# Softmax maxima written to DRAM element by element, and the order of the other tiles moved, in a fused feed-forward/attention kernel

## What is computed (reference, cut)

```
x = x + 0.5 * ffn(layernorm(x))        # 8 experts, top 2, and a shared expert
x = x + attn(layernorm(x))             # 16 heads of 64, see below
x = x + 0.5 * ffn(layernorm(x))
# attn: h = layernorm(x) * ln_scale + ln_bias
#   c_q = h @ w_down_q.T ; c_kv = h @ w_down_kv.T          (128 wide)
#   q, k, v = heads of c_q @ w_up_q.T, c_kv @ w_up_k.T, c_kv @ w_up_v.T ; rotary embedding on q, k
#   out = softmax(q k / 8) v, heads joined, @ w_out.T, + residual
```

## Time and profile before

| | |
|---|---|
| runs (3), device time | 4095.92 us median, 4093.1 to 4099.3 |
| profiled execution, device time | 4098.04 us |
| its span, first to last instruction | 4096.1 us |
| mean granted TensorE clock | 0.988 of full speed |
| busy share of the span | PE 95%, DVE 70%, ACT 62%, POOL 72% |
| DMA | 300.36 MB, 192772 packets |

### The profile page before, as it was taken

How to read it: one execution, slowest core, us unless ns; L and a number is a source line. 1 busy time by engine, 2 the same in 40 slices (tenths; PEclk the granted TensorE clock), 3 DMA queues, 4 the chain that set the end, 5 groups by cost and what they waited for, 6 DMA issues and landing times. The chain is left out here.

```text
span 4096.1 us, 65749 instructions
## 1 busy us (share of the span) xinstructions
PE 3897.4 (95%) x24908; PEld 2207.7 (54%) x24908; DVE 2849.5 (70%) x3796; ACT 2536.2 (62%) x3191; POOL 2932.8 (72%) x1632
## 2 busy tenths in 40 slices
PE   7999979999999999999999999999999999989999
PEld 6888834444444444444444444444444444478888
DVE  5656567777777776777778777767776777565563
ACT  4455446766766676667666766766676666645544
POOL 3444448878877897888788878878887888634443
PEclk9999989999999999999999999999999999999999
DMA  3233221111211221121122212211211121142331
GB/s 123 99 124 109 81 93 53 60 55 59 83 53 53 71 66 53 61 81 53 53 66 76 63 53 66 68 50 60 86 55 53 58 79 62 33 145 76 125 114 63
DMA packets 192772, 300.36 MB, mean 73 GB/s; under 512 B 50328, under 2 KB 100937, under 8 KB 191817
## 3 DMA queue, kind: packets, MB, share of 16 engines
q1 hardware_dynamic: 192456, 296.17, 22.3%
HBM read 201.20 MB, written 26.73 MB: 56 GB/s over the span
## 5 line engine op out<-in xcount | busy, mean ns | idle before, releaser
L1088 DVE TENSOR_REDUCE atNM<-atPS 128x2 f32<-128x1024 f32 x1024 | 1225.7, 1219 | 452.8 <-PE atPS L899 450.1
L1029 ACT ACTIVATE atPT<-atPS 128x1024 f32<-128x1024 f32 x1024 | 1014.0, 1024 | 773.1 <-PE atPS L920 766.7
L1187 POOL TENSOR_TENSOR atACC<-atACC,atPT 128x1024 f32<-128x1024 f32 x510 | 1238.7, 2429 | 89.3 <-ACT atPT L1029 39.1
L931 PE MATMUL atPO<-atPT,atV 128*64 128x512 f32 x4096 | 1014.2, 602 | 0.0
L1187 POOL TENSOR_TENSOR atACC<-atPT 128x1024 f32<-128x1024 f32 x255 | 606.6, 2379 | 262.8 <-PE atOT L953 181.7
L1020 ACT ACTIVATE atPS<-atSH 128x1024 f32<-128x1024 f32 x683 | 687.4, 1023 | 50.8 <-DVE atNM L1088 34.0
L920 PE MATMUL atPS<-atQH,atKL 64*128 64x512 f32 x2048 | 459.9, 445 | 66.3 <-DVE atPS L1094 51.7
L931 PEld LDWEIGHTS atPO<-atPT,atV 128*64 128x64 f32 x4096 | 259.0, 136 | 456.5 <-issue 433.1
L899 PE MATMUL atPS<-atKH,atQH 64*128 64x512 f32 x2048 | 444.0, 431 | 10.0 <-ACT atQH L1009 7.9
L1094 DVE COPY atPS<-atSH 128x1024 f32<-128x1024 f32 x341 | 418.7, 1228 | 37.9 <-DMA atSH<-atMD 11.4
L920 PE MATMUL atPS<-atQH,atKH 64*128 64x512 f32 x2048 | 406.6, 393 | 0.0
(11 more groups left out here) (278 smaller groups left out, 6461.5 us busy)
## 6 DMA issues: line engine op xcount, KB each, us to landing
atSH<-atMD SPq DMA_DIRECT2D x128, 512.0 KB, 4.3
atVT<-atR SPq DMA_DIRECT2D x508, 128.0 KB, 2.1
f1GB<-f1GD SPq DMA_DIRECT2D x128, 256.0 KB, 6.7
f2GB<-f2GD SPq DMA_DIRECT2D x128, 256.0 KB, 6.8
atRSUM<-atRD SPq DMA_DIRECT2D x126, 256.0 KB, 4.0
X<-x SPq DMA_DIRECT2D x4, 1024.0 KB, 6.0
XS<-x SPq DMA_DIRECT2D x16, 256.0 KB, 3.6
x<-X SPq DMA_DIRECT2D x16, 256.0 KB, 2.3
```

What stands on the lines that cost most here:

```text
L931: ins = pe.eng.matmul(PO[HI[h], :], V[n % 2][:, j, HI[h]], PT[k % NPT][:, h, :], start=j == 0, stop=j == T - 1)
L1029: act.eng.activation(PT[k % NPT][:, :, :], PS[ring.of[step]][:, :, :], ACT.Exp, scale=SCALE).then_inc(grown.sem)
L1088: dve.eng.tensor_reduce(NM[:, q // 4, :, q % 4, t], PS[ring.of[step]][:, :, :], AX.X, ALU.max, negate=True).then_inc(most_out.sem)
L1187: pool.eng.tensor_tensor(total[:, :, :], begun[:, :, :], PT[k % NPT][:, :, :], ALU.add).then_inc(gathered.sem)
```

## The change

Four edits, all in `attention`:

1. The step `row` is gone: no transpose on TensorE, no copy by ACT, no tile ML. In its place stands a step `line` of SP alone. It waits for `minus` and for the broadcast that last read the same DRAM line, and issues two DMAs, one for each head of the pair. Each carries MC[:, t, h, :] (128 partitions x 4 elements) to DRAM with partition and column exchanged, 512 separate elements of 4 bytes. `written` counts 32 for a half instead of 16, and `minus` of the next head waits for `written` instead of for the transpose.
2. `apart`: where a `raise` comes in the middle slot of a group of three and the last slot has a use of OT, the raise is moved behind that use (and behind the attends between them), on all engines.
3. TURNS: the two turns of the second half of a batch are moved from periods -9 (early, late) to -13 and -12 (late), the two latents of it from -8 (early, late) to -9 and -8 (late).
4. `others`, the list of the uses of OT, loses `row`.

```
-            TURNS = [(-21, late), (-20, late), (-17, early), (-17, late), (-9, early), (-9, late), (-8, early), (-8, late)]
+            TURNS = [(-21, late), (-20, late), (-17, early), (-17, late), (-13, late), (-12, late), (-9, late), (-8, late)]
...
-                    at(late, m, 5 + 4 * t, ("row", m, t))
+                    at(late, m, 5 + 4 * t, ("line", m, t))
...
+            def uses(steps):
+
+                return [s for s in steps if s[0] in ("turn", "latent", "raise", "value", "sum", "outward")]
+
+            def apart(one, two):
+
+                raised = [s for s in one if s[0] == "raise"]
+                if raised and uses(two):
+                    return [s for s in one if s not in raised], two + raised
+                return one, two
...
-                order += tile("fill", x + 3) + others_of(x + 1) + tile("fill", x + 4) + now + gathers(now) + others_of(x + 2)
+                one, two = apart(others_of(x + 1), others_of(x + 2))
+                order += tile("fill", x + 3) + one + tile("fill", x + 4) + now + gathers(now) + two
...
-                    elif name == "row":
-                        _, n, t = step
-                        free(step)
-                        pe.wait_ge(*minus(n, t))
-                        ins = pe.eng.transpose(OT[0:8, 0:128], MC[:, t, :, :].rearrange("p h q -> p (h q)"), ident[:, :])
-                        ins.then_inc(row.sem)
...
-                    elif name == "row":
-                        _, n, t = step
-                        act.wait_ge(*row(n, t))
-                        act.wait_ge(*written.past(n - 1, t))
-                        act.eng.activation(ML[t][:, :], OT[0:8, 0:128], ACT.Copy).then_inc(row_out.sem)
...
-                        dve.wait_ge(*row.past(n - 1, t))
+                        dve.wait_ge(*written.past(n - 1, t))
...
-                    elif name == "row":
+                    elif name == "line":
                         _, n, t = step
-                        sp.wait_ge(*row_out(n, t))
+                        sp.wait_ge(*minus(n, t))
                         sp.wait_ge(*shift[t].past(n - 2))
-                        sp.eng.dma_start(MD[n % 2][t:t + 1, :].rearrange("o (r i) -> (o r) i", i=128), ML[t][:, :]).then_inc(written.sem, 16)
+                        for h in range(2):
+                            line = MD[n % 2][t:t + 1, h * 512:(h + 1) * 512].rearrange("o (q p) -> (o p) q", p=128)
+                            sp.eng.dma_start(line, MC[:, t, h, :], allow_slow_non_contiguous=True).then_inc(written.sem, 16)
```

More of the change, by code:

```diff
@@ L641, in attention @@
             NM = sb("NM", [128, 2, 2, 4, 2], fp32)
-            MC, ML = sb("MC", [128, 2, 2, 4], fp32), [sb(f"ML{t}", [8, 128], fp32) for t in range(2)]
+            MC = sb("MC", [128, 2, 2, 4], fp32)
             MD = [nc.dram_tensor(f"atMD{i}", [2, 2 * 512], fp32, kind="Internal").ap() for i in range(2)]
@@ L730, in attention @@
                 order += tile("score", x) + most_of(x) + tile("fill", x + 2) + tile("score", x + 1)
-                order += others_of(x) + held + tile("attend", x - 1)
-                order += gathers(held + tile("attend", x - 1))
+                now = held + tile("attend", x - 1)
+                order += others_of(x) + now + gathers(now)
                 order += most_of(x + 1) + tile("score", x + 2) + most_of(x + 2)
@@ L778, in attention @@
             minus = sig("minus").expect(halves)
-            row, row_out = sig("row").expect(halves), sig("rowo").expect(halves)
-            written = sig("written", 16).expect(halves)
+            written = sig("written", 32).expect(halves)
             shift = [sig(f"shift{t}", 16).expect(heads) for t in range(2)]
@@ L809, in earlier @@
                 return (k // T // 2, k // T % 2, k % T) if k >= 0 else None
-            others = [s for s in order if s[0] in ("turn", "latent", "raise", "value", "row", "sum", "outward")]
+            others = [s for s in order if s[0] in ("turn", "latent", "raise", "value", "sum", "outward")]
             first = others[:12]
@@ L828, in attention @@
             FREED = {"turn": hidden, "latent": latent_out, "raise": cosine, "value": value_out,
-                     "row": row_out, "outward": added,
+                     "outward": added,
                      "sum": lambda n, t: sum_out(n, t) if n < NN - 1 else ended(t, "inverse")}
```

## The result

| | before | after |
|---|---|---|
| device time, median | 4097.01 us (4 runs, 4093.1 to 4099.3) | 4906.35 us (4 runs, 4899.13 to 4917.76) |
| span of the profiled execution | 4096.1 us | 4897.1 us |
| mean granted TensorE clock | 0.988 | 0.917 |
| DMA packets | 192772 | 325889 |

The ratio is 1.1978, with a 95% interval of 1.196 to 1.1997. The change makes the kernel a fifth slower; forecast were 4084 us, in a range of 4062 to 4106.

A forecast was written before the change was run, and what follows sets the result against it. TensorE's own instructions, busy 193.4 of 200 us and broken by short waits, were taken to set the pace. From 4098.0, -20 - 4 + 11 + 1 = -12 gave 4086, so 4084 us for the median; range 4062 to 4106.

The forecast's parts named there:

- 0.6 + 1.8 + 60 x 0.020 = 3.6 us: Element DMAs' landing: issue, plus a 4 KB write, plus 60 further packets per engine at 20 ns (12 to 45).
- The estimate of 10.8 us: Element DMAs: 1024 packets at about 10.5 ns each from the skill's table, too late for all halves; set aside.
- Rival (c): Elements land late and fills wait for SH: slower above 40 ns a packet, 4160 us at 70 ns; chance 0.09.
- the tight third: The 40 to 46 of 128 halves with least time from maxima to first fill, leaving elements 4.8 us.
- The transpose: Removing TensorE's 128 transposes of 0.20 us each: -20 us, between 17.6 and 25.6 saved.
- rival (b): PE's saved 0.20 us per transpose is swallowed at the next fill wait: 4090 to 4102 us; chance 0.20.
- Part 2: Raises moved behind the other use: 20 behind a sum wait for ACT's copy instead of DVE, +11 us.
- Part 3: Moved turns and latents, with 10 raises behind a turn: +1 us in sum, from -8 to +10.
- the term of -11: The 14 turns no longer wait behind an `outward`: -11.1 us.
- the one of +12: The 10 raises behind a turn wait for ACT's copy of it, 1.2 us each: +12 us.
- What would show it: Signs expected in the profile after: transpose gone, broadcast 3.5 to 4 us after maxima, changed waits of fills, sums, raises, turns.
- The third named line that makes me wrong: Last of three stated signs that the forecast is wrong: fills in the attention stage wait for SH.

The follow-up runs named there:

- z1: Kernel before plus 1024 extra 4-byte element writes into an unread DRAM buffer, 64 bytes apart, broadcast waiting for them: 4120.40 us, ratio 1.0052.
- y3: Kernel before plus 1024 extra 4-byte element writes into an unread DRAM buffer, 512 bytes apart, broadcast waiting for them: 4114.85 us, ratio 1.0042.
- z3: Kernel before plus 128 extra 4-byte element writes, dense, into an unread DRAM buffer, broadcast waiting for them: 4522.13 us, ratio 1.1032.
- z2: Kernel before plus 1024 extra 4-byte element writes into an unread DRAM buffer, 16 bytes apart, broadcast waiting for them: 4189.26 us, ratio 1.0219.
- y4: Kernel before plus 1024 extra dense 4-byte element writes into an unread DRAM buffer, broadcast not waiting for them: 4842.72 us, ratio 1.1824.
- y1: Kernel before plus 1024 extra dense 4-byte element writes into an unread DRAM buffer, broadcast waiting for them: 4844.55 us, ratio 1.1828.
- e1: Changed kernel with the old order of raises, turns and latents, so element DMAs alone against the kernel before: 4841.44 us, ratio 1.1825.
- w2: No TensorE transpose, old order; DVE turns the padded maxima in 32 x 32 blocks, four DMAs write 8 rows each: 4091.31 us, ratio 0.9991.
- e2b: Kernel before, transpose kept, with only the raises moved behind the other uses: 4113.18 us, ratio 1.0048.
- e2c: Kernel before, transpose kept, with only the turns and latents moved: 4085.13 us, ratio 0.9974.
- e2: Kernel before, transpose kept, with raises, turns and latents all in the new order: 4117.32 us, ratio 1.0055.
- e7: No transpose, old order; every fourth query forms a block of the maxima's product, two DMAs write 256 rows of 16 bytes: 4129.73 us, ratio 1.0087.
- e5: No transpose, old order; one DMA writes 128 rows of 32 bytes and fills read SH with a stride: 4546.30 us, ratio 1.1110.

## Why the prediction was wrong

**What failed is one term of the sum**: "0.6 + 1.8 + 60 x 0.020 = 3.6 us, from 3.1 (12 ns) to 5.1 (45 ns)". Measured were 10.6 us from the first issue to the broadcast. Not the price of a packet was off: busy time in the trace after gives 7.7 ns each, below the 12 of the earlier trace rows. The form of the term was wrong. It let every engine work off its 64 packets at its own rate, with nothing between them but their number. What took the time was their address: sixteen 4-byte writes into the same 64 bytes, from sixteen packets. z1 and y3 show it: the same packets go to other places, each DMA lands 2.0 to 2.1 us after its issue (median), even below the 3.1 to 5.1 of the term, and only 20 us of the price remain. The range was built from rows that couldn't hold this case: none of the writes I read there puts more than one packet into 64 bytes, so neither end of "12 to 45 ns" bounded it from above, and I should have kept the upper end open.

**The estimate of 10.8 us.** It took about 10.5 ns a packet from the Trainium skill (DMA: Bandwidth & Descriptors, Bandwidth), a figure for loads of 64 packets from DRAM, and I argued it away by the engines' busy time. As a warning it was right, and so was the rule of the Trainium skill (DMA: Bandwidth & Descriptors, Rules for kernel authors) against a transpose by a rearranged access pattern. As an explanation it is not: a price of 10.5 ns for each packet in series would give 1024 spread elements the same 10.8 us, and 128 dense ones 1.3. Measured are 2.0 us for each of the two DMAs of y3, and 7.4 us for z3. That the sum with it comes near the 10.6 us is luck.

**Rival (c)** named the mechanism behind it rightly (fills wait for SH, the tight third first), at a chance of 0.09 and with a price of 70 ns a packet as its worst. At 10.6 us more than the tight third is late: 161 fills waited for SH, in 119 of the 128 halves. The condition of the rival, 4.8 us to spare, fits the runs: z2's elements stay near it (the last lands 3.4 to 5.6 us after the first issue) and cost 2%, z3's 7.4 us cost 10%.

**What I left out** comes with long waits: the clock, by the estimate above the 184 of the 801 us that are busy time, and what stands behind the elements in the queue. "The elements are done before they are issued" was said of the swaps; POOL waits 369 us for them (51.8 before), and y4 shows a write behind the elements done late though nothing but its own completion is waited for. The prediction did count the swaps among what SP issues later, but took for granted that they go out free.

**The transpose** (-20 us) could not be read in the changed kernel. y1 has transpose and elements, e1 elements alone: 4844.55 and 4841.44 us (1.1828 and 1.1825 of their kernels before), less apart than their intervals of 8 us to either side. That PE waits for fills anyway would explain it. Beside a way of turning that doesn't hold up the fills, w2, 3 us came through. That looks like rival (b), swallowed by the waits for fills, though w2 also adds work of its own; what the transpose is worth without any such work no run shows.

**Part 2** (+11) measured 19 to 20 alone (e2b). The mechanism was as described: the wait for DVE goes, the wait for ACT comes, 20 times. The 19.6 us between the spans are 10.1 of idle time (-31.6 for DVE, +35.9 for atRSUM, +7.7 for atHT, -1.3 at the turns) and 9.5 of busy time (3906.9 against 3897.4 us) at a mean clock of 0.986 instead of 0.988. So waits alone would have been +10, near the +11; the sum had nothing for busy time. That new idle time costs clock would explain the other 9.5, but it is not shown: runs of the kernel before differ by as much as 0.986 to 0.991 among themselves. The bound I gave, up to 20, held.

**Part 3** (+1) measured -10 alone (e2c), for the term of -11 at the turns was right and the one of +12, for raises behind a turn, does not come without the moved raises. It comes with them, 8 us in e2b and 18 in e2, so it was put to the wrong part and too small. Parts 2 and 3 together were forecast at +12 and measured +22.

**What would show it**: no transpose and no copy into ML, yes; the broadcast 3.5 to 4 us after the maxima, no, 10.6 in the second halves and 13.7 in the first; no wait of a fill for SH over 1 us, no, up to 13.6, and 34.2 at the first fill of the stage; the wait of the sum for atU gone and one of `raise` for atRSUM 20 times, yes, at 1.6 us each; for atHT, 17 times instead of 10; turns without a wait for X, yes. The third named line that makes me wrong, fills waiting for SH, is what happened.

## What to carry to other kernels

A DMA that turns data by writing single elements next to each other pays far more for the neighbourhood of its writes than for their number: ask how many of them fall into the same 64 bytes of DRAM, and write rows instead (of 16 bytes in e7, of 32 in e5, both without this price). Busy time of the DMA engines doesn't show it; the landing does, or the distance from the issue to who waited for it, and a write behind such a DMA in its queue can be late with it. Where no row of a trace shows an access of that kind, the nearest rows don't bound it from above; put a probe beside the kernel (as y1: same DMA, a buffer that nobody reads) before the way that works is taken out, and measure two moves in an order together as well as one by one.

## What was unexpected in the hardware

- Dense 4-byte writes to DRAM, from the maxima to the broadcast that waits for them: about 7.4 us for 128, 9.1 for 512 and 10.5 for 1024. Spread at 64 or 512 bytes, two DMAs of 512 take 2.0 to 2.1 us each to land, at 16 bytes 3.2. As an estimate, what each further write into the same 64 bytes adds is (7.4 - 1.24) / 15 = 0.4 us from z3 and (3.2 - 2.1) / 3 = 0.4 us from z2 and z1.
- It is not the number of writes in 64 bytes alone. e7 puts four rows of 16 bytes there, as many as z2 has elements, and its DMAs land in 1.7 us (median); e5, with two rows of 32 bytes, in 1.6. Whether the size of a write or the number of packets (128 against 512 a DMA) makes that difference is not separated, nor whether writes of one DMA engine or of several hold each other up. The size of the piece is only bracketed, over 16 and not over 64 bytes, and that it is a read before each write, or anything else, was not tested.
- A small write issued 6 us behind such elements in the same queue took 4.5 us instead of 1.24, though its own packets were over within 0.9 us of its issue (y4).
- A copy of 128 x 1024 fp32 from SBUF to PSUM with a stride of 32 bytes takes 2.08 us, on ACT (1.02 without) and on DVE (1.23) alike (e5); a weight load with a stride of 16 bytes takes 306 ns, 185 without (e7).
